# Tokenizer of a vision tower: spectra kept by mode and placed by GpSimd, first convolution on 64-row tiles, columns folded by GpSimd

## What is computed

```python
h = jnp.concatenate([grid, x], axis=-1) @ P_w + P_b
h = jnp.transpose(h, (0, 3, 1, 2))
for i in range(nl):
    h_ft = jnp.fft.rfft2(h)
    w_c = spec_wr[i] + 1j * spec_wi[i]
    out_modes = jnp.einsum('bixy,ioxy->boxy', h_ft[:, :, :mx, :my], w_c)
    spec = jnp.fft.irfft2(out_modes, s=(H, W))
    conv = lax.conv_general_dilated(h, conv_w[i], (1, 1), 'SAME', dimension_numbers=dn)
    conv = conv + conv_b[i][None, :, None, None]
    h = leaky(spec + conv)
h = jnp.transpose(h, (0, 2, 3, 1))
h = leaky(h @ Q1_w + Q1_b)
out = (h @ Q2_w + Q2_b)[..., 0]
```

## Time and profile before

| | |
|---|---|
| median of 3 runs | 7531.51 us (7525.21 to 7532.25) |
| the profiled execution | 7536.45 us |
| its span | 7534.4 us |
| PE busy | 6726.4 us, 89% |
| PE weight loads busy | 3991.5 us, 53% |
| DVE busy | 4995.7 us, 66% |
| ACT busy | 2567.0 us, 34% |
| POOL busy | 61.3 us, 1% |
| DMA moved | 568.39 MB, mean 75 GB/s |

### The profile page before, as it was taken

The page is one execution under the profiler, slowest core; times in us unless marked ns, Lnnn a source line. Parts: engine busy times, 40 slices in busy tenths (PEclk is TensorE's granted clock), DMA queues, the critical chain, the costliest instruction groups (busy, mean ns, idle before and its releaser), DMA issues. The chain is left out here.

```text
span 7534.4 us, 262144 instructions
## 1 busy us (share of the span) xinstructions
PE 6726.4 (89%) x107382; PEld 3991.5 (53%) x107382; DVE 4995.7 (66%) x7931; ACT 2567.0 (34%) x4418; POOL 61.3 (1%) x47
## 2 busy tenths in 40 slices
PE   5699998999999899999989999758888888888888
PEld 4466666666666666666654444334434444344443
DVE  3599995777777477777667777664545555455454
ACT  1244442333333233333223333233343333433333
POOL 1000000000000000000000000000000000000000
PEclk8899998999999899999999999879999999999999
DMA  6444444444444444444432222200000000000000
GB/s 155 113 124 129 125 124 134 125 124 118 123 124 110 138 118 124 124 118 123 117 100 77 77 76 75 86 6 1 3 1 3 3 1 3 2 2 3 1 3 2
DMA packets 655549, 568.39 MB, mean 75 GB/s; under 512 B 328096, under 2 KB 527904, under 8 KB 649126
## 3 DMA queue, kind: packets, MB, share of 16 engines
q1 hardware_dynamic: 655176, 563.43, 28.2%
HBM read 315.77 MB, written 247.61 MB: 75 GB/s over the span
## 5 line engine op out<-in xcount | busy, mean ns | idle before, releaser
L548 PE MATMUL abank<-inv_basis,mode_tile 128*32 128x128 f32 x32768 | 1013.6, 276 | 94.6 <-DMA mode_tile<-m_img 66.4
L594 PE MATMUL zbank<-rows_in,conv_taps 64*32 64x512 f32 (+1 forms) x18432 | 1049.7, 588 | 0.0
L548 PEld LDWEIGHTS abank<-inv_basis,mode_tile 128*32 128x32 f32 x32768 | 877.3, 111 | 269.4 <-issue 269.4
L954 DVE SCALAR_TENSOR_TENSOR rows_out<-zbank,conv_bias,work 128x1024 f32<-128x1024 f32 x512 | 633.7, 1279 | 516.9 <-PE zbank L603 504.9
L816 ACT ACTIVATE turned<-tbank 128x1024 f32<-128x1024 f32 x400 | 410.2, 1026 | 1550.9 <-PE tbank L617 1550.9
L810 ACT ACTIVATE inv_copy<-abank 128x1024 f32<-128x1024 f32 x512 | 524.4, 1024 | 776.4 <-PE abank L548 776.4
L632 PE MATMUL zbank<-fwd_basis,turned 128*64 128x128 f32 x12288 | 760.2, 277 | 19.9 <-ACT turned L816 13.1
L930 DVE TENSOR_TENSOR work<-inv_copy 128x512 f32<-128x512 f32 x1024 | 653.6, 684 | 164.1 <-ACT inv_copy L810 163.8
L632 PEld LDWEIGHTS zbank<-fwd_basis,turned 128*64 128x64 f32 x12288 | 668.6, 137 | 97.7 <-issue 97.7
L603 PE MATMUL zbank<-rows_in,conv_taps 32*32 32x512 f32 (+1 forms) x18432 | 702.5, 593 | 0.0
L594 PEld LDWEIGHTS zbank<-rows_in,conv_taps 64*32 64x32 f32 x18432 | 329.5, 106 | 583.0 <-issue 583.0
(11 more groups left out here) (367 smaller groups left out, 7091.2 us busy)
## 6 DMA issues: line engine op xcount, KB each, us to landing
h_rows<-rows_out SPq DMA_DIRECT2D x768, 256.0 KB, 4.1
rows_in<-h_rows SPq DMA_DIRECT2D x384, 512.0 KB, 4.9
m_img<-rows_out SPq DMA_DIRECT2D x32, 1024.0 KB, 5.3
mode_tile<-m_img SPq DMA_DIRECT2D x512, 64.0 KB, 3.1
rows_in<-x_pad SPq DMA_DIRECT2D x384, 48.7 KB
rows_out<-x_pad SPq DMA_DIRECT2D x384, 48.7 KB
tokens<-spectra SPq DMA_DIRECT2D x512, 4.0 KB
weights<-in_weights SPq DMA_DIRECT2D x1, 6060.0 KB, 19.5
```

What stands on the lines that cost most here:

```text
L548: last = nc.tensor.matmul(ab[32 * p:32 * p + 32, s, 128 * k:128 * k + 128], mode_tile[u][:, k, a, :], inv[:, k, s, 128 * p:128 * p + 128], ...
L594: nc.tensor.matmul(section(zb[32 * p:32 * p + 32, 2 * a + so, :])[:, :, :, out], conv_t[part, dx, so, :], moving(part, p, 0, src), start=( ...
L954: nc.vector.scalar_tensor_tensor(out=rows_out[u][:, half].rearrange("p (s x) -> p s x", s=2), in0=zb[:, 2 * a:2 * a + 2, :], scalar=conv_b ...
```

## The change

It has five parts.

1. `g_img` is now `spectra` seen as "p (m n)": mode after mode, the 128 images of one mode together. Everything that writes it does so with a step of 128 elements.
2. `modes_copy` on ACT is one copy of 256 columns into a new tile `placed`; GpSimd (`place`) then makes the eight copies of 32 x 128 into `g_img`, and the mix waits for `g_placed`. ACT's copy of a pair waits until the pair before it is placed.
3. `fold_cols` of the layers moves from DVE to GpSimd, with the same operations and the same waits. The eight tiles of the opening are still folded by DVE.
4. The first layer's convolution has a row group of 64 rows for each sublattice, 54 of them used (3 shifts of 9 rows of x and 9 of the grid). Its 16 matmuls use 64 rows x 32 columns each; the wait for `g_ready` now stands between the two images and not between the sublattices. The loads of `x_rows` are still twelve, with 54 rows together in place of 36; those of the grid rows are six in place of three. The weights `x_conv` are computed by six small matmuls, and nine small loads of constants go.
5. In `sp_mix` the weights of parts 1 to 3 of the first mix are issued ahead of all, and those of part a + 3 right behind the store of part a - 1, for a = 1 to 4.

```diff
-        g_img = spectra[:].rearrange("p (n m) -> p n m", n=IMGS)
+        g_img = spectra[:].rearrange("p (m n) -> p n m", n=IMGS)
+        placed = sb("placed", [128, 2 * MX * MY // 2])
...
-            part, at = slice(32 * r, 32 * r + 32), 3 * r
+            part, at = slice(32 * r, 32 * r + 32), 36 + 3 * r
-            for k in range(3):
-                load(embed_t[part, at + k:at + k + 1], column(embed_w[2 + k, :]))
-            for k in range(2):
-                load(embed_t[part, at + 12 + k:at + 13 + k], column(embed_w[k, :]))
-            load(embed_t[part, at + 14:at + 15], column(embed_b))
+            if r < 3:
+                for k in range(3):
+                    load(embed_t[part, at + k:at + k + 1], column(embed_w[2 + k, :]))
+                for k in range(2):
+                    load(embed_t[part, at + 9 + k:at + 10 + k], column(embed_w[k, :]))
+                load(embed_t[part, at + 11:at + 12], column(embed_b))
...
-                for so in range(2):
-                    for dy in range(3):
-                        load(conv_bd[32 * (so + dy):32 * (so + dy) + 32, :, 32 * so:32 * so + 32],
-                             conv_w[0, dy, :, :, :].rearrange("c x o -> c x o"))
-            assert loads == (11, 15, 9, 9)[r]
-        NLATE = 11 + 15 + 9 + 9
+                for dy in range(3):
+                    load(conv_bd[32 * dy:32 * dy + 32, :, :], conv_w[0, dy, :, :, :].rearrange("c x o -> c x o"))
+            assert loads == (11, 12, 9, 3)[r]
+        NLATE = 11 + 12 + 9 + 3
...
-                at = 32 * dx + 12
-                sp.dma_start(x_rows[u][at:at + 12, :, 0:SPAN],
-                             grid_slots.rearrange("r k x -> (r k) x")[:, dx:dx + SPAN].unsqueeze(1).broadcast_to([12, 2, SPAN])).then_inc(grid_rows_in[u], 16)
+                for s in range(2):
+                    at = 64 * s + 18 * dx + 9
+                    sp.dma_start(x_rows[u][at:at + 9, :, 0:SPAN],
+                                 grid_slots[s:s + 3, :, dx:dx + SPAN].rearrange("r k x -> (r k) x").unsqueeze(1).broadcast_to([9, 2, SPAN]))\
+                        .then_inc(grid_rows_in[u], 16)
-                for r in range(4):
-                    at, start = 32 * dx + 3 * r, ROW_START[r] + dx
-                    sp.dma_start(x_rows[u][at:at + 3, :, 0:SPAN],
-                                 x_pad[bass.ds(2 * n, 2), ROW_SET[r], :, start:start + SPAN].rearrange("a c x -> c a x"))\
+                for s in range(2):
+                    at = 64 * s + 18 * dx
+                    alone, both = (at, at + 3) if s == 0 else (at + 6, at)
+                    start = (0, 2 * PITCH)[s] + dx
+                    sp.dma_start(x_rows[u][alone:alone + 3, :, 0:SPAN],
+                                 x_pad[bass.ds(2 * n, 2), 1 - s, :, start:start + SPAN].rearrange("a c x -> c a x"))\
+                        .then_inc(x_rows_in[u], 16)
+                    sp.dma_start(x_rows[u][both:both + 6, :, 0:SPAN],
+                                 x_pad[bass.ds(2 * n, 2), :, :, PITCH + dx:PITCH + dx + SPAN].rearrange("a r c x -> (r c) a x"))\
...
+            if kind == "first":
+                for a in range(1, 4):
+                    sp_load_weights(sp, l, a)
-                if a >= 4 or (a >= 1 and kind == "first"):
-                    sp_load_weights(sp, l, a)
+                if 1 <= a <= 4:
+                    sp_load_weights(sp, l, a + 3)
...
-            nc.gpsimd.memset(x_conv[:], 0.0).then_inc(zeroed, 1)
+            def place(n, l):
+                pool.wait_ge(g_ready, ET + PAIRS * l + n + 1)
+                pool.nop(nofuse=True)
+                for x in range(2):
+                    for a in range(2):
+                        at = 64 * x + 32 * a
+                        for r in range(2):
+                            part = slice(64 * x + 32 * r, 64 * x + 32 * r + 32)
+                            image = g_img[part, 2 * n + a, :] if isinstance(n, int) else \
+                                g_img[part, bass.ds(2 * n + a, 1), :].rearrange("p n m -> p (n m)")
+                            last = nc.gpsimd.tensor_copy(image, placed[at:at + 32, 128 * r:128 * r + 128])
+                last.then_inc(g_placed, 1)
+            def fold_cols(g):
+                pool.wait_ge(rows_folded, g + 1)
+                pool.nop(nofuse=True)
+                v = by_row[:].rearrange("p x (j v w) -> p (x j) v w", v=2, w=COLS // 2)
+                for y, op in ((0, ALU.add), (1, ALU.subtract)):
+                    need(pool, flip_done, 2 * g + y - 1)
+                    nc.gpsimd.tensor_tensor(folded[:, y, :, :, :].rearrange("p x b (j w) -> p (x b j) w", w=COLS // 2),
+                                            v[:, :, 0, :], v[:, :, 1, :], op).then_inc(cols_folded, 1)
+            def layer(l):
+                need(pool, g_placed, PAIRS * l)
+                fold_cols(ET + PAIRS * l)
+                pool.wait_ge(cols_folded, 2 * (ET + PAIRS * l + 1))
+                fold_cols(ET + PAIRS * l + 1)
+                pool.wait_ge(cols_folded, 2 * (ET + PAIRS * l + 2))
+                place(0, l)
+                with looped(pool, 2, PAIRS) as n:
+                    pool.wait_ge(g_placed, PAIRS * l + n - 1)
+                    fold_cols(ET + PAIRS * l + n)
+                    pool.wait_ge(cols_folded, 2 * (ET + PAIRS * l + n) + 2)
+                    place(n - 1, l)
+                pool.wait_ge(cols_folded, 2 * (ET + PAIRS * l + PAIRS))
+                place(PAIRS - 1, l)
+            layer(0)
+            with pool.Fori(1, LAST) as l:
+                layer(l)
...
-                pe_need(pe, grid_rows_in[u], 48)
-            for s in range(2):
-                if s == 1:
+                pe_need(pe, grid_rows_in[u], 96)
+            for a in range(2):
+                if a == 1:
-                for a in range(2):
-                    planes_of = x_rows[u][:, a, 0:J * PITCH].rearrange("p (h q j w) -> p q h j w", h=2, q=4, w=PITCH)
-                    for p in range(4):
-                        last = nc.tensor.matmul(section(zb[32 * p:32 * p + 32, 2 * a + s, :]), x_conv[:, 32 * s:32 * s + 32],
-                                                planes_of[:, p, :, :, 0:COLS], start=True, stop=True)
+                planes_of = x_rows[u][:, a, 0:J * PITCH].rearrange("p (h q j w) -> p q h j w", h=2, q=4, w=PITCH)
+                for p in range(4):
+                    for s in range(2):
+                        part = slice(64 * s, 64 * s + 54)
+                        last = nc.tensor.matmul(section(zb[32 * p:32 * p + 32, 2 * a + s, :]), x_conv[part, :],
+                                                planes_of[part, p, :, :, 0:COLS], start=True, stop=True)
...
+                    pe_need(pe, g_placed, PAIRS * l)
...
-            for dx in range(3):
-                last = nc.tensor.matmul(ab[32 * dx:32 * dx + 32, 0, 0:64], embed_t[:], conv_bd[:, dx, :],
-                                        start=True, stop=True)
+            for s in range(2):
+                for dx in range(3):
+                    last = nc.tensor.matmul(ab[64 * s:64 * s + 54, 0, 0:32], embed_t[0:96, 36 - 18 * dx:90 - 18 * dx],
+                                            conv_bd[0:96, dx, :], start=(dx == 0), stop=(dx == 2))
...
-                act.nop(nofuse=True)
-                for x in range(2):
-                    for a in range(2):
-                        at = 64 * x + 32 * a
-                        for r in range(2):
-                            part = slice(64 * x + 32 * r, 64 * x + 32 * r + 32)
-                            image = g_img[part, 2 * n + a, :] if isinstance(n, int) else \
-                                g_img[part, bass.ds(2 * n + a, 1), :].rearrange("p n m -> p (n m)")
-                            last = nc.scalar.activation(image, gb[at:at + 32, 128 * r:128 * r + 128], ACT.Identity)
-                last.then_inc(g_ready, 1)
+                need(act, g_placed, PAIRS * l + n)
+                nc.scalar.activation(placed[:], gb[:, 0:256], ACT.Identity).then_inc(g_ready, 1)
...
-                            at = 128 * (32 * g + 4 * i)
-                            last = nc.scalar.activation(spectra[:, at:at + CH], xbank[i % 2][g], ACT.Identity)
+                            at = 32 * g + 4 * i
+                            last = nc.scalar.activation(g_img[:, at:at + 4, :], xbank[i % 2][g].rearrange("p (n m) -> p n m", n=4),
+                                                        ACT.Identity)
...
-                    nc.scalar.activation(x_conv[0:96, :], ab[0:96, 0, 0:64], ACT.Identity).then_inc(x_conv_ready, 1)
+                    for s in range(2):
+                        part = slice(64 * s, 64 * s + 54)
+                        last = nc.scalar.activation(x_conv[part, :], ab[part, 0, 0:32], ACT.Identity)
+                    last.then_inc(x_conv_ready, 1)
...
-                fold_cols(ET + layers + n)
...
-                            at = 128 * (32 * g + 4 * i)
```

(13 more changed lines are left out.)

## The result

The changed kernel takes 7555.61 us (median of 20 runs, 7544.12 to 7572.13) against 7537.27 us for the kernel before in the same comparison (20 runs, 7525.21 to 7550.83). The ratio is 1.0024, 95% interval [1.0016, 1.0032]. The profiled execution has a span of 7542.0 us. The forecast was 7502 us, that is faster, with 7440 to 7545 as the range of its likeliest case; the kernel became 0.24% slower.

What follows compares the result with a forecast made beforehand. DVE was taken to bound the first layer (14.09 us a pair), PE layers 1 and 2. 7531.5 + 95 (pairs) - 95 (middle mixes) - 36 (first mix) + 6 (small) = 7501.5, about 7502 us; range 7255 to 7600.

Steps and rivals of the forecast that it cites:

- case A: First layer: GpSimd's folds and DVE's two-input reads exclude each other, with overlap under new_rows; 15.6 us a pair, 7502; chance 0.42.
- rival D: First layer: POOL and DVE alternate instructions behind fold_rows, nearly nothing under new_rows; 16.8 us a pair, 7574; chance 0.18.
- step (3): First layer's folds and copies on GpSimd: 11.82 + 4.4 + 1.6 - 2.2 = 15.6 us a pair, +95 us over some 62 pairs.
- the overlap under new_rows: First layer: new_rows has one SBUF input, so POOL can read beside it; 2.2 us a pair subtracted.
- the exclusion: First layer: a GpSimd SBUF read and a two-input DVE instruction exclude each other, the second waiting in full; folds 4.4, copies 1.6 us.
- (1): fold_cols leaves DVE in the first layer: DVE's pair falls by 2.27 us, from 14.09 to 11.82.
- (2): First layer's convolution on 64-row tiles: 1.8 to 1.9 us in place of 3.85, PE's pair 11.5 us.
- (4): Mixes read the stationary operand by mode, elements together: a part takes 3.7 us of PE in place of 7.20.
- step (5): SP's new order in the mixes: middle ones 48 us in place of 79.6, -95 for three; first mix -36.
- step (6): Small ones: folds and placing at layer ends, +6 us; the expansion's strided writes 0 to +8, taken at 0.
- the cover: Layers 1 and 2: 3.65 us idle and 2.27 freed on DVE against at most 6.0; nothing lost, pair stays 18.28 us.

Runs made afterwards that it cites:

- e4: The kernel before with one edit, the layers' column folds moved from DVE to GpSimd: 7666.5 us, ratio 1.0153.
- e3: The changed kernel with the eight placing copies back on ACT, GpSimd only folding: 7708.97 us, ratio 1.0216.
- e2: The changed kernel with each GpSimd fold replaced by three memsets, so GpSimd's folds only write: 7369.72 us (one run).
- e8: The changed kernel with a pair's first fold on DVE, the second on GpSimd after a wait for spectral_rows, beside new_rows: 7379.68 us, ratio 0.9774.
- e1: The changed kernel with the layers' column folds back on DVE, GpSimd only placing: 7433.74 us, ratio 0.9847.
- e11: e1 with ACT making eight copies side by side and GpSimd two copies of 128 x 128 in place of eight: 7403.87 us, ratio 0.9819.
- e7: The kernel before with only the changed kernel's 64-row convolution of the first layer and its loads: 7536.27 us, ratio 0.9991.
- e6: The kernel before with only SP's new order of weight loads in the mixes: 7468.26 us, ratio 0.989.
- e10: e8 with ACT making eight copies side by side and GpSimd two copies of 128 x 128 in place of eight: 7348.34 us, ratio 0.9738.

## Why the prediction was wrong

**The verdict.** The forecast was case A (15.6 us a pair, 7502). What happened is rival D, by its own mechanism: 16.8 us a pair and 7574 were its numbers; 16.75 as the typical period and 7555.6 us were measured. The step that failed is step (3), in its overlap of 2.2 us under new_rows, and with it the chance of 0.42 for A against 0.18 for D. That D's 16.8 fits within 0.1 us is in part luck: D took 1.0 us off its 17.8 without a reason, and the terms below show that the copies cost 1.5 us less and a wait that D did not have 0.9 us more.

**Step (3), the exclusion: right.** DVE is held for whole instructions by GpSimd's reads (e4 and e3, and 1366 ns in the mean for `inverse_sums` in place of 684), not by its writes (e2), and new_rows with one SBUF input isn't held (e8). By the Trainium skill, SBUF — State Buffer, section "Who interferes with whom", a VectorE instruction with two SBUF inputs contends with a GpSimd instruction that reads SBUF, not with one that only writes, and whoever comes second waits in full. The runs agree: 5.08 us beside 5.13 us of folds, 1.29 us beside memsets, and 2.48 us for new_rows, with one SBUF input, beside a fold of 2.38. The wait can also be longer than one instruction of the other engine: 5.29 us for a copy in e1. The rival theory, that the convolution, the copies or the hand-over from ACT make the pair longer, doesn't hold: e1 and e11 keep all three and lose nothing or 0.5 us a pair, and e4 has none of them and loses 2.2.

**Step (3), the overlap under new_rows: wrong.** I subtracted 2.2 us because GpSimd may read beside new_rows. But nothing made it wait for that. The fold is ready when `fold_rows` ends, and between `fold_rows` and new_rows stand four instructions of DVE that read twice. Both folds had ended 3.2 us before new_rows began (606.17 against 609.34). A place where two engines can overlap is worth nothing unless the waits put the work there; e8 puts it there with one wait.

**Step (3), the terms.** Against the 15.6 us of the sum:

- overlap under new_rows: 2.2 expected, 0 measured: +2.2.
- the folds: 4.4 expected to fall on DVE. They take 2.36 and 2.8 us, but the first starts 0.61 us before DVE's next instruction, and that part costs nothing. From start to start `inverse_sums` takes 5.11 us (601.65 to 606.76) in place of 1.21, 3.9 lost: -0.5.
- the copies: 1.6 expected on DVE's path. They take 0.66 us each in the mean (5.26 for eight, 0.40 where nothing holds them; I had 0.11 to 0.28 as bounds, which was too low), but it is they that wait: `spectral_rows` take 2.58 us from 606.76 to 609.34, and 2.48 or 2.59 in turn in the kernel before (415.33 to 417.81, 401.13 to 403.72): 0.1 lost at most, -1.5.
- a wait that the sum didn't have: DVE waits 0.83 us for ACT's `inv_copy`, and its next instruction no longer overlaps the one before: +0.9.

15.6 + 2.2 - 0.5 - 1.5 + 0.9 = 16.7 us. The overlap alone decides: without it the sum of step (3) would have read 17.8 us, which is where D started; with it and the other three terms as measured it would have read 14.5 us, 62 x 0.4 = 25 us over the first layer of before, and the kernel would have become faster.

**Where the 0.83 us come from.** The row at 610.77 shows PE idle for 3.57 us before the forward transform, since new_rows comes late, and then 2.87 us for 32 records that take 1.97 elsewhere; the flips behind it take 1.81 in place of 1.09. The windows view of the kernel after, core 0 (us, busy of PE, PEld, DVE, ACT, POOL, then the granted clock, the DMA share and GB/s):

```profile
603.00:607.00 4.00, 4.00 (x98) 2.85 (x88) 3.97 (x3) 1.03 (x1) 3.76 (x3) 1.00 0.36 73
...
612.00:614.00 2.00, 2.00 (x18) 1.67 (x15) 2.00 (x2) 0.00 (x0) 0.00 (x0) 0.50 0.21 62
614.00:616.00 2.00, 2.00 (x34) 1.83 (x36) 2.00 (x4) 0.58 (x1) 0.00 (x0) 0.73 0.54 147
```

The granted clock is 1.00 before the gap and 0.50, the lower level of 1.2 GHz, behind it. Forward transform and flips lose 0.90 + 0.72 = 1.6 us, the inverse transform and ACT's copy come that much later, and DVE waits 0.83 us.

What the lower clock costs is read from the same trace. In 13 of the 62 pairs that follow the first one, forward transform and flips ran at a granted clock of 1.00, although in 7 of these PE had waited 3.6 or 3.7 us just before. In none of the 13 does DVE wait for `inv_copy`, and they take 16.3 us in the mean; in the other 49 the clock was 0.63 to 0.67 there, DVE waits 0.5 to 0.9 us in every one, and they take 16.8. One of the 13 in the timeline of the kernel after:

```profile
343.79 1.97 PE L687 MATMUL zbank<-fwd_basis,turned 128*64 128x128 f32 x32 [3.63 <-DVE rows_out L1007]
...
350.81 6.49 POOL L566 TENSOR_TENSOR folded<-by_row 128x1024 f32<-128x1024 f32 x2 [6.11 <-DVE by_row L1024]
351.82 3.24 DVE L992 TENSOR_TENSOR work<-work 128x1024 f32<-128x1024 f32 x1
...
354.98 3.40 DVE L993 TENSOR_TENSOR work<-work 128x1024 f32<-128x1024 f32 x1
```

Without the wait DVE's `inverse_sums` comes before the fold, and the folds hold `spectral_rows` instead, as in e4 (16.25 us a pair). So the clock costs 0.5 us of the pair and not the whole 0.83, and at full clock the pair would still be 2.2 us over the 14.1 of before: the lower clock is not the reason of the loss.

**Steps (1) and (2): right and worth little.** DVE was relieved of 2.27 us a pair, which the folds' 3.9 took back. The convolution takes 1.95 us for both halves (1.8 to 1.9 estimated), and by itself brings nothing (e7).

**Steps (4) and (5): right for the middle mixes.** 3.74 us a part (3.7 predicted), -30.6, -30.0 and -30.4 a mix (-31.6). The value given for the order alone, 11 us, was measured in e6 as 11.8. For the first mix -36 was predicted and -44.9 measured; that the stage shows -39.5 is because the opening became 5.4 us longer, which step (6) had allowed for (0 to 8) and taken at 0. The near hit is luck in a second way too: the working of step (5), 50.5 us less half of 20.7 us added twice, gives -30 and not -36.

**Step (6) and the cover in layers 1 and 2.** The cover held: DVE's idle time before new_rows fell from 3.65 us to 1.54, still behind PE:

```profile
1859.97 5.35 DVE L983 TENSOR_TENSOR work<-inv_copy 128x512 f32<-128x512 f32 x2 [0.58 <-ACT inv_copy L867]
...
1869.34 2.48 DVE L1007 SCALAR_TENSOR_TENSOR rows_out<-zbank,conv_bias,work 128x1024 f32<-128x1024 f32 x2 [1.54 <-PE zbank L658]
```

`inverse_sums` is held here as in the first layer (5.35 us), and it costs nothing. The prediction named as a sign of being wrong that these layers leave 18.28 us. They did by 0.1 us: the pair takes 18.18 us in the kernel after, e1, e2 and e8, where ACT makes one copy, 18.28 in the kernel before, e4, e6 and e7, where it makes eight, and 18.21 in e10 and e11, eight with the elements side by side. So it goes with ACT's copies and not with the folds; why they cost PE this much was not tested.

**The whole.** With the measured stages in place of the predicted ones, and nothing for the rest, the sum is 7531.5 + 167.7 - 91.0 - 39.5 - 11.5 = 7557 us, and 7555.6 was measured. From the median of before in the same comparison, 7537.3, it is 7563, 7 us over.

## What to carry to other kernels

Moving a step from VectorE to GpSimd relieved VectorE only where GpSimd's reads lay beside VectorE instructions with at most one SBUF input. Look at what VectorE executes from the moment the moved step becomes ready, not at where it could fit, and place it there with a wait: both folds on GpSimd as they came ready cost 133 us against none (the changed kernel against e1), one placed beside new_rows gained 48 us (e1 to e8) or 56 (e11 to e10), each against the kernel before beside it. Where GpSimd moves data in small copies, count the copies and not their partitions.

## What the hardware showed that was not expected

- A GpSimd copy of 128 elements takes 0.41 us when DVE leaves it alone, on 32 partitions (e8) as on 128 (e10). Beside a DVE that reads twice without pause it waits for DVE: 0.93 us in the mean on 32 partitions (e8, 300 to 1050 us), 1.33 on 128 (e10), and 5.29 us for a single one in e1. The eight take 5.26 us in the changed kernel, 7.78 in e8 and 9.17 in e1.
- GpSimd's memset of 128 x 1024 elements takes 0.95 to 1.0 us, its addition or subtraction of the same size 2.38 us undisturbed (e8) and 2.64 us in the mean after.
- ACT's writes to SBUF with a step of 128 elements cost 3.15 us for eight copies (e3), 2.22 without it.
- PE's weight loads with a step of 128 elements set 7.20 us a part against 3.74 with the elements side by side (for the same 32 records), as e6 and the changed kernel show, which in the mixes differ in this step. The Trainium skill, SBUF — State Buffer, section "Door 1: The DMA port swizzle", in its note on cachelines, says that each access which crosses to a new line of 16 bytes pays a penalty; a step of 512 bytes does so with every element, and these two kinds of access agree, at 1.9 and 1.4 times.
- Behind a wait of 3.4 to 4.1 us PE ran at half its clock for a part of the next two groups of matmuls in 49 pairs of the first layer, and behind one of 3.6 or 3.7 us at full clock in 7.
